# Emptying steps of a pipelined RWKV and FP4 layer: the x rounding moved in between the links of the gated values' rounding

## The chip, the cores and the metric

One NeuronCore of a Trainium2 chip runs the whole kernel. The metric is device time in microseconds of one launch. The engines are TensorE (PE), VectorE (DVE), ScalarE (ACT), GpSimd (POOL) and SyncE (SP), which issues the loads and stores. Each works off its own queue in program order, and semaphores tie them together.

## The reference

The input `x` is 4 sequences of 1024 tokens with 256 channels. Cut to what matters:

```
xx = shifted(x) - x
r, k, v = (x + xx * mix_r) @ W_r.T, (x + xx * mix_k) @ W_k.T, (x + xx * mix_v) @ W_v.T
g = sigmoid((x + xx * mix_g) @ W_g.T)
attn = linear recurrence over tokens of r, k, v with a decay per channel (16 heads of 16)
x1 = layernorm(x + layernorm(attn * g @ W_o.T) * gamma + beta)
xq = fp4(x1)                                  # blocks of 16 channels share max|x| / 6
h  = silu(xq @ fp4(w_gate).T) * (xq @ fp4(w_up).T)      # 704 wide
out = layernorm(x1 + fp4(h) @ fp4(w_down).T)
```

`fp4` divides by the block's scale, rounds to the eight magnitudes 0, 0.5, 1, 1.5, 2, 3, 4, 6 with the sign, and multiplies by the scale.

## The kernel before

The 4096 tokens are 32 tiles of 128 tokens (eight of a sequence). A software pipeline works on one stage of each of nine tiles per step: `run_tiles` calls each engine's `step` 40 times (g = 0 to 39), and in step g `tile(lag)` is tile g - lag, or None outside 0 to 31. The order inside a step is written out by hand for every engine, with the waits in front of each operation. There is no planner. The branch that runs here has `general` false, so `ffn` is 1.

The stages that matter here, by lag: 2 the scores (ACT copies them, POOL masks them in the next step, L410); 3 the attention output, gating by `gate_heads` (DVE L1355), the output projection (PE L919); 4 first norm (`norm1`), `centred`, `residual`, second norm (`norm2`), the roots on POOL (`rstd_of`, L392 and L404), and x1 on ACT (L597); 5 the rounding of x1 (`xgrid`) and its scaling on POOL (`scale_x`, L419); 6 the transposes of `xq` (PE L931), the split in a high and a low part (ACT L627, DVE L1324 `low_x`), gate and up matmuls (PE L855), SiLU (ACT L594) and the product (`gated`, DVE L1286); 7 the rounding of the product (`hgrid`), its scaling on POOL (`hq`, L462), its transposes (PE L956) and copies to SBUF (ACT L665, L667); 8 the down projection (PE L967), `add_x1` (DVE L1317), the last norm (`norm3`), its root, the output (ACT) and the store.

A rounding is a chain of seven links in `grid`, each waiting for the one before it: 0 block maximum (L1067), 1 scale (L1069), 2 reciprocal (L1071), 3 scaled values (L1073), 4 magnitude (L1076), 5 add (L1079), 6 subtract (L1081). For x1 the operands are 128x256 (scales 128x16), for the gated product 128x704 (scales 128x44). All the tiles that they use (`x_grid`, `x_mag`, `late`, which holds `hid`, `h_grid`, `h_mag` and `sig_h`) lie in SBUF.

Gate and up are done in halves of 352 columns, each in one bank: gate half 0, up half 0, gate half 1, up half 1 on PE. Up half 1 overwrites the bank that `gated(0)` reads, so PE waits for `hid_step` before it; `gated(1)` waits for up half 1. Link 0 of the next step's `hgrid` waits for `gated(1)`, and x link 0 waits for `x1_ready` of its tile, which ACT gives at the end of the step before.

A step is emptying (`draining`) when tiles 0 and 1 are None: steps 33 to 39. There `step` of DVE takes a list of its own, ACT does `gate(t, 1)` ahead of the `hq_t` copies and x1, and PE starts with the `xq` transposes and the down projection. x tiles 28 to 31 are rounded in steps 33 to 36. The last tile's product is rounded in two halves (`last_grid`, POOL L474). In an emptying step before the change, DVE does all x links behind `gated(0)`, and POOL's order is: masks, `xb` (L448), root 0, `hq`, root 2 (last norm), the last tile's halves, root 1 (x1), x scaling.

Of the kernel before, what the change touches and what calls it, by code (L numbers as in the profile page):

```python
# [35 lines left out]
TAB, LN, LN2, QN = 11, 8, 4, 7  # L36
# [20 lines left out]
def wait(eng, sem, value):  # L57

    if isinstance(value, int) and value <= 0:
        return  # L60
    eng.wait_ge(sem, value)
# [60 lines left out]
def build(nc, x, time_decay, mix_k, mix_v, mix_r, mix_g, w_r, w_k, w_v, w_g, w_o, gamma, beta,  # L122
          w_gate, w_up, w_down, out):
    with ExitStack() as ctx:
# [176 lines left out]
        def per_block(ap, n):  # L301
            return ap[:, 0:n].unsqueeze(2).broadcast_to([ap.shape[0], n, BLK])
# [63 lines left out]
        def _(pool):  # L366
# [20 lines left out]
            def rstd_of(t, i, general):  # L387
                wait(pool, ln_step if i < 2 else ln2_step, t.count(LN if i < 2 else LN2,
                                                                  (3, 8, 4)[i]))
                if i:  # L390
                    wait(pool, x1_ready if i == 1 else y_ready, t.count(1, 0))
                g.tensor_tensor(rstd[:, i:i + 1], veps[:, i:i + 1], neg_half, ALU.pow  # L392
                                ).then_inc((rstd_ready, x_rstd, y_rstd)[i], 1)
                if i:
                    ready = x_norm_ready if i == 1 else rstd2_ready
                    wait(pool, (rstd_ready, x_rstd, y_rstd)[i], t.count(1, 1))
                    if general:
                        g.tensor_tensor(nmr[:, i:i + 1], mv[:, i, 0:1], rstd[:, i:i + 1], ALU.mult
                                        ).then_inc((rstd_ready, x_mean, y_mean)[i], 1)
                        wait(pool, (rstd_ready, x_mean, y_mean)[i], t.count(1, 1))  # L400
                        g.tensor_tensor(nmr[:, i:i + 1], nmr[:, i:i + 1], minus, ALU.mult
                                        ).then_inc(ready, 1)
                    else:
                        g.tensor_scalar(nmr[:, i:i + 1], mv[:, i, 0:1], rstd[:, i:i + 1], -1.0,  # L404
                                        ALU.mult, ALU.mult).then_inc(ready, 1)
# [16 lines left out]
            def step(tile, general):  # L422
                ffn = 0 if general else FFN
                t = None if general else tile(3)
                if t is not None:
                    wait(pool, mixed, t.count(4, 12))
                    mask(t, 0)
                    mask(t, 1)
                    mask(t, 2)
                    mask(t, 3)  # L430
                t = tile(0)
                if t is not None:
                    wait(pool, x_t_ready, t.count(1, 1))
                    wait(pool, mixed, t.count(4, -4))
                    g.tensor_tensor(shift[:, t.c % 2], x_t[:, t.c % 2, :, 0:P],  # L435
                                    x_t[:, t.c % 2, :, 1:P + 1], ALU.subtract).then_inc(shifted, 1)
                    if not general and t.b == 0 and 1 <= t.c <= 4:
                        for n in range(2 * t.c - 2, min(2 * t.c, len(pieces))):
                            dequantize(n)
                        if t.c == 4:  # L440
                            pad_hidden()
                t = tile(4)
                if t is not None:
                    if t.first():
                        pool.wait_ge(norm_loaded, 16 * 2)
                    wait(pool, x_in[t.c], t.affine(16, 16))
                    wait(pool, ln_step, t.count(LN, 5 - 2 * LN))
                    g.tensor_tensor(xb[:, t.c % 2], x_tok[:, t.c], beta_b, ALU.add  # L448
                                    ).then_inc(xb_ready, 1)
                t = tile(4)  # L450
                if t is not None:
                    rstd_of(t, 0, general)
                drain = draining(tile, general)
                t = tile(7 + ffn)
                if t is not None and not drain:
                    rstd_of(t, 2, general)
                t = tile(6 + ffn)
                if t is not None and not (is_last(t) and drain):
                    wait(pool, hquant_step, t.count(QN, QN))
                    wait(pool, h_tr, t.count(1, -1))  # L460
                    nb = HID // BLK
                    g.tensor_tensor(blocks(hq[:, t.c % 2, 0:HID], nb), blocks(h_grid, nb),  # L462
                                    per_block(h_scale, nb), ALU.mult).then_inc(hq_ready, 1)
                t = tile(7 + ffn)
                if t is not None and drain:
                    rstd_of(t, 2, general)
                t = tile(5 + ffn)
                if is_last(t) and drain:
                    wait(pool, h_tr, t.count(1, -1))
                    nb = HH // BLK  # L470
                    for half in range(2):
                        pool.wait_ge(last_step[half], QN)
                        part = slice(half * HH, (half + 1) * HH)
                        g.tensor_tensor(blocks(hq[:, t.c % 2, part], nb), blocks(h_grid[:, part], nb),  # L474
                                        per_block(h_scale[:, half * nb:(half + 1) * nb], nb), ALU.mult
                                        ).then_inc(last_ready, 1)
                t = tile(4)
                if t is not None:
                    rstd_of(t, 1, general)
                if not general:  # L480
                    scale_x(tile(5), general)
                if general:
                    scale_x(tile(4), general)
# [562 lines left out]
        def _(dve):  # L1046
# [160 lines left out]
            def step(tile, general):  # L1207
# [28 lines left out]
                def hgrid(k):  # L1236
                    if t6 is None or is_last(t6) and not general:
                        return
                    if k == 0:
                        wait(dve, hid_step, t6.count(2, 2))  # L1240
                        wait(dve, hq_ready, t6.count(1, 0))
                    grid(k, hid, h_grid, HID // BLK, h_scale, h_inv, h_mag, hquant_step,
                         lambda i: t6.count(QN, i))
# [16 lines left out]
                def norm1(k):  # L1260
                    if t4 is not None:
                        if k == 0:
                            wait(dve, wo_done, t4.count(1, 1))
                        norm(k, B_S0[:, 0:C], 0, ln_step, t4, 1)
# [47 lines left out]
                def add_x1():  # L1312

                    if t7 is not None:
                        wait(dve, down_done, t7.count(1, 1))
                        wait(dve, y_ready, t7.count(1, 0))
                        v.tensor_tensor(u2, B_PA[:, 0:C], x1[:, t7.c], ALU.add).then_inc(ln2_step, 1)  # L1317
# [11 lines left out]
                def centred():  # L1329

                    if t4 is not None:
                        v.scalar_tensor_tensor(u1, B_S0[:, 0:C], mv[:, 0, 0:1], gamma_b,
                                               ALU.subtract, ALU.mult).then_inc(ln_step, 1)
# [60 lines left out]
                if draining(tile, general):  # L1394
                    if t2 is not None:
                        add_x1()
                    hgrid(0)
                    norm1(0)
                    hgrid(1)
                    norm1(1)  # L1400
                    hgrid(2)
                    norm1(2)
                    centred()
                    low_x()
                    hgrid(3)
                    residual()
                    gate_heads()
                    hgrid(4)
                    if t2 is None:
                        add_x1()  # L1410
                    norm2(0)
                    hgrid(5)
                    norm3(0)
                    norm2(1)
                    hgrid(6)
                    norm3(1)
                    norm2(2)
                    norm3(2)
                    next_state(0)
                    gated(0)  # L1420
                    last_grid(0)
                    xgrid(0)
                    next_state(1)
                    xgrid(1)
                    next_state(2)
                    for k in range(2, QN):
                        xgrid(k)
                    gated(1)
                    last_grid(1)
                    return  # L1430
# [144 lines left out]
```

## Time and profile before

| | us |
|---|---|
| three timed runs, median (lowest to highest) | 569.05 (568.41 to 571.27) |
| profiled execution | 567.12 |
| its span, first to last instruction | 565.3 |
| busy: TensorE matmuls | 515.4 (91%) |
| busy: VectorE | 507.7 (90%) |
| busy: GpSimd | 286.6 (51%) |
| busy: ScalarE | 260.1 (46%) |
| mean granted TensorE clock | 0.980 of full |

The shares are means over the whole span; a step in the full part takes about 15.4 us and is not touched by the edit. The emptying steps begin at about 495 us. A timeline row gives the start in us, the duration, the engine, the line, what is written and read, and in brackets how long the engine had been idle and who released it.

### The profile page before, as it was taken

How to read it: one execution, taken by the hardware profiler on the slowest of the kernel's cores; microseconds unless marked ns; L12 is line 12 of the kernel's file. 1: busy time of each engine (PE TensorE's matmuls, PEld its weight loads, DVE VectorE, ACT ScalarE, POOL GpSimd, SP SyncE). 2: the span in 40 equal slices, each digit the busy share in tenths (PEclk: the TensorE clock that was granted, in tenths of full speed). 3: DMA queues.
4: the chain of work that ended last, by engine and by line, in shares of the span. 5: the costliest groups of instructions: out<-in, count | busy, mean ns of one | idle time of the engine just before them, and what ended most of it. 6: DMA issues, size and time to landing. Idle time of an engine off the chain costs nothing.

```text
span 565.3 us, 14795 instructions
## 1 busy us (share of the span) xinstructions
PE 515.4 (91%) x5120; PEld 448.8 (79%) x5120; DVE 507.7 (90%) x1535; ACT 260.1 (46%) x614; POOL 286.6 (51%) x439
## 2 busy tenths in 40 slices
PE   2758789899999999999999999999999999988783
PEld 1647578788888888889888888888888988867672
DVE  7998578999999999999999999999999999799982
ACT  3426454445554444554554555444455454532221
POOL 3246453455566555555555555555565554554321
PEclk9969899999999999999999999999999999999997
DMA  7300000000000000000000000000000000000000
GB/s 211 129 1 2 11 11 10 1 22 20 20 21 21 20 20 20 5 18 20 20 20 21 20 20 20 20 21 20 11 12 20 10 11 12 12 10 11 10 20 23
DMA packets 14046, 13.14 MB, mean 23 GB/s; under 512 B 2576, under 2 KB 13712, under 8 KB 13968
## 3 DMA queue, kind: packets, MB, share of 16 engines
q1 hardware_dynamic: 13968, 12.13, 6.9%
q8 instruction: 45, 0.74, 0.5%
q14 instruction: 33, 0.27, 0.2%
HBM read 7.93 MB, written 4.19 MB: 21 GB/s over the span
## 4 chain that ended last, share of the span: by engine, by line
issue 45%; POOL 42%; DVE 8%; PE 3%; ACT 1%; POOLq 0%; DMA 0%; DVEq 0%; ACTq 0%
POOL scores L410 12%; POOL rstd L392 11%; POOL hq L462 8%; POOL nmr L404 4%; POOL shift L435 3%; POOL xb L448 2%; DVE mix L1222 2%; POOL xq L419 1%; PE bank L967 1%; PE bank L794 1%; DVE q_scale L1067 1%; ACT scores L589 1%; PE bank L919 1%; DVE hq L1079 0%; DVE hq L1073 0%
## 5 line engine op out<-in xcount | busy, mean ns | idle before, releaser
L589 ACT COPY scores<-bank 128x512 f32<-128x512 f32 x128 | 68.3, 593 | 72.0 <-PE bank L794 72.0
L462 POOL TENSOR_TENSOR hq<-late,h_scale 128x704 f32<-128x704 f32 x31 | 43.2, 1392 | 96.2 <-DVE late L1081 96.2
L967 PE MATMUL bank<-down_t,hq_t 128*128 128x256 f32 x384 | 89.9, 384 | 1.5 <-ACT hq_t L665 1.5
L410 POOL TENSOR_SCALAR_AFFINE_SELECT scores<-scores 128x512 f32<-128x512 f32 x128 | 80.8, 669 | 10.2 <-ACT scores L589 10.2
L967 PEld LDWEIGHTS bank<-down_t,hq_t 128*128 128x128 f32 x384 | 72.7, 193 | 10.8 <-issue 2.0
L1222 DVE SCALAR_TENSOR_TENSOR mix<-shift,mu,x_t 128x128 f32<-128x128 f32 x256 | 78.9, 355 | 1.3 <-POOL shift L435 1.3
L419 POOL TENSOR_TENSOR xq<-x_grid,x_scale 128x256 f32<-128x256 f32 x32 | 19.9, 622 | 113.0 <-DVE x_grid L1081 113.0
L392 POOL TENSOR_TENSOR rstd<-veps,neg_half 128x1 f32<-128x1 f32 x96 | 65.3, 690 | 19.0 <-DVE veps L1169 19.0
L855 PE MATMUL bank<-gu_hi,xq_hi 128*128 128x352 f32 x256 | 71.2, 359 | 2.6 <-DVE late L1286 2.6
L891 PE MATMUL bank<-mix,proj_t 128*128 128x128 f32 x512 | 66.1, 284 | 0.0
L891 PEld LDWEIGHTS bank<-mix,proj_t 128*128 128x128 f32 x512 | 61.1, 196 | 3.2 <-issue 1.1
L855 PE MATMUL bank<-gu_hi,xq_lo 128*128 128x352 f32 x256 | 61.7, 322 | 0.0
L855 PE MATMUL bank<-gu_lo,xq_hi 128*128 128x352 f32 x256 | 61.6, 322 | 0.0
L855 PEld LDWEIGHTS bank<-gu_hi,xq_hi 128*128 128x128 f32 x256 | 43.9, 188 | 14.8 <-issue 9.5
L1286 DVE TENSOR_TENSOR late<-late,bank 128x352 f32<-128x352 f32 x64 | 33.0, 516 | 19.6 <-PE bank L855 19.4
L532 ACT COPY x_t<-bank 128x256 f32<-128x256 f32 x32 | 12.0, 375 | 82.8 <-PE bank L704 82.8
L594 ACT ACTIVATE late<-bank 128x352 f32<-128x352 f32 x64 | 29.7, 465 | 37.6 <-PE bank L855 34.7
L794 PE MATMUL bank<-r_par,rv 32*128 32x256 f32 x512 | 37.6, 408 | 9.6 <-DVE kd L1389 7.3
L855 PEld LDWEIGHTS bank<-gu_lo,xq_hi 128*128 128x128 f32 x256 | 44.5, 188 | 0.0
L855 PEld LDWEIGHTS bank<-gu_hi,xq_lo 128*128 128x128 f32 x256 | 44.5, 188 | 0.0
L633 ACT COPY rv<-bank 128x512 f32<-128x512 f32 x32 | 18.8, 586 | 47.9 <-PE bank L891 47.9
L919 PE MATMUL bank<-proj_t,attn 128*128 128x256 f32 x128 | 34.2, 391 | 4.1 <-ACT scores L589 4.0
(128 smaller groups left out, 1131.4 us busy)
## 6 DMA issues: line engine op xcount, KB each, us to landing
x_tok<-in_L_attn_x_dram SPq DMA_DIRECT2D x32, 128.0 KB, 2.2
out_dram<-late_down SPq DMA_DIRECT2D x32, 128.0 KB, 1.7
late_down<-in_L_ffn_w_down_dram SPq DMA_DIRECT2D x1, 704.0 KB, 7.9
late<-in_L_ffn_w_gate_dram SPq DMA_DIRECT2D x1, 640.0 KB, 4.5
late<-in_L_ffn_w_up_dram SPq DMA_DIRECT2D x1, 640.0 KB, 6.6
scores<-in_L_attn_W_r_dram SPq DMA_DIRECT2D x1, 256.0 KB, 4.5
scores<-in_L_attn_W_v_dram SPq DMA_DIRECT2D x1, 256.0 KB, 4.6
scores<-in_L_attn_W_g_dram SPq DMA_DIRECT2D x1, 256.0 KB, 4.9
```

The costliest lines, as they stand in the source:

```text
L392: g.tensor_tensor(rstd[:, i:i + 1], veps[:, i:i + 1], neg_half, ALU.pow).then_inc((rstd_ready, x_rstd, y_rstd)[i], 1)
L410: g.affine_select(out=a, in_=a, compare_op=ALU.is_ge, fill=0.0, base=0, pattern=[[0, 4], [1, P]], channel_multiplier=-1).then_inc(s_masked, 1)
L462: g.tensor_tensor(blocks(hq[:, t.c % 2, 0:HID], nb), blocks(h_grid, nb), per_block(h_scale, nb), ALU.mult).then_inc(hq_ready, 1)
L589: s.copy(scores[:, t.c % 2, 4 * q:4 * q + 4, :], src).then_inc(s_moved, 1)
L594: s.activation(sig_h[:, i], B_GATE[:, 0:HH], ACT.Silu).then_inc(sig_ready, 1)
L794: mm = t_.matmul(s_bank[q][:, hf * 256:hf * 256 + 256], rv[rows, t.c % 4, 1, hf], r_par[rows, t.c % 2, hf].rearrange("p r n -> p (r n)"), ...
L855: mm = t_.matmul(b[:, 0:HH], x[:, t.c % 2, k], w[:, k, o + i * HH:o + (i + 1) * HH], start=(n == 0), stop=(n == len(parts) - 1))
L891: mm = t_.matmul(B_PA[:, o:o + P], proj_t[:, i, k, m * P:(m + 1) * P], mix[:, t.c % 2, i, k], start=(k == 0), stop=(k == KC - 1))
L919: mm = t_.matmul(B_S0[:, 0:C], attn[:, t.c % 2, k], proj_t[:, 4, k], start=(k == 0), stop=(k == KC - 1))
L967: mm = t_.matmul(B_PA[:, 0:C], hq_t[:, t.c % 2, j], down_t[:, j], start=(j == 0), stop=(j == NH - 1))
L1222: ins = v.scalar_tensor_tensor(mix[:, t0.c % 2, i, k], shift[:, t0.c % 2, k], mu[:, i, k:k + 1], x_t[:, t0.c % 2, k, 1:P + 1], ALU.mult, A ...
L1286: v.tensor_tensor(hid[:, i * HH:(i + 1) * HH], sig_h[:, i], B_UP[:, 0:HH], ALU.mult).then_inc(hid_step, 1)
```

## The change

Two edits, both only in emptying steps. On DVE the seven x links no longer follow `gated(0)` in a row; they stand one by one between the links of `hgrid`, and `gate_heads`, the norms and the state update shift a little against each other. On POOL the x scaling comes directly behind `hq`, then x1's root, then the last norm's root, then the last tile's halves. In full steps the order of both engines stays what it was.

```diff
@@ gpsimd step
                     g.tensor_tensor(blocks(hq[:, t.c % 2, 0:HID], nb), blocks(h_grid, nb),
                                     per_block(h_scale, nb), ALU.mult).then_inc(hq_ready, 1)
+                if drain:
+                    scale_x(tile(5), general)
+                t = tile(4)
+                if t is not None:
+                    rstd_of(t, 1, general)
                 t = tile(7 + ffn)
                 if t is not None and drain:
                     rstd_of(t, 2, general)
...
-                t = tile(4)
-                if t is not None:
-                    rstd_of(t, 1, general)
-                if not general:
+                if not general and not drain:
                     scale_x(tile(5), general)
@@ vector step, draining
                     hgrid(1)
                     norm1(1)
+                    xgrid(0)
                     hgrid(2)
                     norm1(2)
+                    xgrid(1)
                     centred()
+                    xgrid(2)
                     low_x()
                     hgrid(3)
                     residual()
+                    xgrid(3)
+                    hgrid(4)
+                    xgrid(4)
                     gate_heads()
-                    hgrid(4)
                     if t2 is None:
                         add_x1()
+                    hgrid(5)
+                    xgrid(5)
                     norm2(0)
-                    hgrid(5)
+                    hgrid(6)
+                    norm2(1)
                     norm3(0)
-                    norm2(1)
-                    hgrid(6)
+                    xgrid(6)
+                    norm2(2)
                     norm3(1)
-                    norm2(2)
+                    next_state(0)
                     norm3(2)
-                    next_state(0)
+                    next_state(1)
                     gated(0)
                     last_grid(0)
-                    xgrid(0)
-                    next_state(1)
-                    xgrid(1)
                     next_state(2)
-                    for k in range(2, QN):
-                        xgrid(k)
                     gated(1)
                     last_grid(1)
```

## Rows read from the trace of the kernel before

**Rows 1.** Windows, steps 33 to 36: length; PE, PEld, DVE, ACT, POOL busy; clock; DMA.
```profile
495.14:506.08 10.94, 8.68 (x111) 7.26 (x98) 10.77 (x36) 4.32 (x10) 4.41 (x7) 1.00 0.00 0
506.08:518.81 12.73, 10.69 (x112) 9.01 (x112) 11.78 (x34) 3.24 (x8) 8.14 (x13) 1.00 0.04 12
518.81:529.57 10.76, 7.80 (x44) 6.94 (x44) 10.52 (x33) 3.23 (x8) 5.16 (x9) 1.00 0.05 14
529.57:539.25 9.68, 7.80 (x44) 6.94 (x44) 9.13 (x23) 3.30 (x8) 2.83 (x5) 1.00 0.04 14
```

**Rows 2.** Timeline of PE: second up half, and the head of step 36.
```profile
526.44 0.59 PE L855 MATMUL bank<-gu_hi,xq_hi 128*128 128x352 f32 x2 [1.42 <-DVE late L1286]
...
529.87 0.44 PE L931 MATMUL bank<-ident,xq 128*128 128x128 f32 x2 [1.55 <-POOL xq L419]
```

**Rows 3.** Timeline, step 36: gate and up on PE, transposes, copies.
```profile
532.55 0.67 PE L855 MATMUL bank<-gu_hi,xq_hi 128*128 128x352 f32 x2
...
536.11 0.59 PE L855 MATMUL bank<-gu_hi,xq_hi 128*128 128x352 f32 x2 [0.33 <-DVE late L1286]
...
536.85 0.49 PE L855 MATMUL bank<-gu_hi,xq_lo 128*128 128x352 f32 x2
537.18 0.82 PE L956 MATMUL bank<-ident,hq 128*128 128x128 f32 x6
...
538.03 0.59 ACT L665 COPY hq_t<-bank 128x512 f32<-128x512 f32 x1 [1.75 <-PE bank L956]
```

**Rows 4.** Timeline of DVE (one row POOL), step 35 and two of step 36.
```profile
524.76 0.85 DVE L1081 SCALAR_TENSOR_TENSOR late<-late 128x704 f32<-128x704 f32 x1
...
525.70 1.39 POOL L462 TENSOR_TENSOR hq<-late,h_scale 128x704 f32<-128x704 f32 x1 [4.46 <-DVE late L1081]
...
525.86 0.52 DVE L1286 TENSOR_TENSOR late<-late,bank 128x352 f32<-128x352 f32 x1
526.30 0.41 DVE L1067 TENSOR_REDUCE x_scale<-x 128x16 f32<-128x256 f32 x1
...
528.68 0.42 DVE L1081 SCALAR_TENSOR_TENSOR x_grid<-x_mag,x_grid 128x256 f32<-128x256 f32 x1
529.02 0.51 DVE L1286 TENSOR_TENSOR late<-late,bank 128x352 f32<-128x352 f32 x1
...
535.54 0.52 DVE L1286 TENSOR_TENSOR late<-late,bank 128x352 f32<-128x352 f32 x1
```

**Rows 5.** Timeline, DVE and POOL: `s_half` free, then steps 33 and 34.
```profile
489.22 0.16 DVE L1374 TENSOR_TENSOR s_half<-s_part,half_decay 128x64 f32<-128x64 f32 x1
...
502.02 1.39 POOL L462 TENSOR_TENSOR hq<-late,h_scale 128x704 f32<-128x704 f32 x1 [4.47 <-DVE late L1081]
...
503.04 0.45 DVE L1374 TENSOR_TENSOR s_half<-s_part,half_decay 128x64 f32<-128x64 f32 x1
503.41 0.17 DVE L1069 TENSOR_SCALAR x_scale<-x_scale 128x16 f32<-128x16 f32 x1
...
508.66 0.73 POOL L448 TENSOR_TENSOR xb<-x_tok,beta_b 128x256 f32<-128x256 f32 x1
508.67 1.46 DVE L1073 SCALAR_TENSOR_TENSOR late<-late,h_inv 128x704 f32<-128x704 f32 x1
510.64 0.48 DVE L1342 SCALAR_TENSOR_TENSOR u<-u,rstd,xb 128x256 f32<-128x256 f32 x1 [0.51 <-POOL rstd L392]
```

**Rows 6.** Timeline of POOL, step 35: the x scaling.
```profile
529.20 0.62 POOL L419 TENSOR_TENSOR xq<-x_grid,x_scale 128x256 f32<-128x256 f32 x1
```

**Rows 7.** Windows at the end of the run, then PE's down projections.
```profile
551.50:554.10 2.60, 0.00 (x0) 0.00 (x0) 2.42 (x8) 0.00 (x0) 0.79 (x1) 1.00 0.00 0
...
556.00:559.50 3.50, 3.50 (x11) 2.73 (x10) 0.00 (x0) 0.20 (x1) 0.00 (x0) 0.52 0.13 42
...
530.14 2.76 PE L967 MATMUL bank<-down_t,hq_t 128*128 128x256 f32 x12
...
555.57 4.52 PE L967 MATMUL bank<-down_t,hq_t 128*128 128x256 f32 x12 [0.77 <-ACT hq_t L665]
```

## The prediction

> **What bounds the kernel now.** I first cut the seven emptying steps out of the page's long span, because only they run the edited code, and only four of them (I call them 33 to 36) hold an x rounding at all. In [rows 1] the reader sees one row per step, from the first link of the gated values' rounding to the next. VectorE (DVE) is busy 10.77 of 10.94 us, 11.78 of 12.73, 10.52 of 10.76 and 9.13 of 9.68, while TensorE (PE) has 1.9 to 3 us of slack in each step and GpSimd (POOL) more. So DVE's own queue sets the step; a wait of PE counts only if DVE later waits for PE. PE does wait 1.55 us for `xq` at the head of a step [rows 2], and that is the wait which the edit takes away. But step 36 runs on without it: what PE waits for next is DVE's first gated product (line 1286) [rows 3].
>
> The second thing to see is the order inside a DVE step [rows 4]: `gated(0)` at 525.86, then the seven x links (526.30 to 529.1), then `gated(1)` at 529.02, and 0.55 us later (529.57 by [rows 1]) the next step's first link. `gated(0)` to `gated(1)` is 3.16 us. Under those x links PE makes its return trip: `gated(0)` frees the bank of the up half, PE does six matmuls from 536.11 to 537.34 [rows 3] and only then may `gated(1)` read them. From 535.54, when `gated(0)` starts, to 537.38 that is 1.84 us, all of it hidden by the x rounding today.
>
> **The change, part by part.** Times are start to start on DVE. Two neighbours that don't depend on each other start about 0.08 us before the former's recorded end (0.41 long, 0.33 apart), a dependent one about 0.03 after it.
>
> 1. *x links go ahead of `gated(0)`.* Seven links of 0.41, 0.17, 0.25, 0.42, 0.29, 0.43 and 0.42 us [rows 4, 5] (0.17 is the second link's duration in the latter) less 7 x 0.08 are about 1.82 us a step, four steps: +7.3. In steps 33 to 35 the h chain is already filled with norms, so no gap absorbs them. In step 36 the h links stand almost alone; 0.27 us of gaps close there: -0.3.
>
> 2. *The x links leave the place behind `gated(0)`.* The interval falls from 3.16 to the return trip of 1.84: -1.32 in three steps, and -1.42 in step 33, which has 3.26. Sum -5.4. This is the cover that is gone: without the return trip the gain would have been up to 2.7 us a step. Parts 1 and 2 alone are +1.6.
>
> 3. *The last x link meets `hq` on GpSimd.* This is the largest term. POOL starts `hq` (L462, 1.39 us) 0.09 us after the last h link ends [rows 4]. In the new order the next DVE work is two small norm operations, of one input each, and then x link 6, which reads two SBUF tensors (`x_mag`, `x_grid`). The trace shows what such an operation does beside a POOL operation on data [rows 5]: `s_half`, 0.16 us when free, took 0.45 and ended 0.08 after `hq` did; h link 3, of two inputs, took 1.46 instead of 0.88 and ended 0.74 after `xb` did. Both look as if they had started about 0.1 before POOL's operation ended. So x link 6, wanted 0.35 us after the last h link (H), starts at H + 1.38: +1.03 in steps 33 to 35 and +1.10 in 36, where one norm operation less stands between: +4.2. Bounds: zero if the two rows have another cause, 1.2 a step (all of `hq`) above. I take 1.03, because two different pairs fit it within 0.1. In step 33 `s_half` now stands ahead of `gated(0)` and meets POOL's x scaling (0.62 [rows 6]): +0.35 by the same reading.
>
> The Trainium skill, "SBUF — State Buffer", section "Who interferes with whom", says that a DVE operation with two SBUF inputs contends with a GpSimd operation that reads SBUF, and that whichever starts first keeps the shared ports for its whole length while the other waits. By that rule term 3 stands as worked out, and the trace agrees with it (0.45 against 0.16).
>
> 4. *GpSimd's order.* The x scaling (0.62 [rows 6]) moves from behind two root pairs to ahead of them. `xq` is ready before PE wants it, which by [rows 1] buys nothing. x1's root comes later by the scaling but earlier by the swap with the last norm's; ScalarE reaches x1 only behind the `hq_t` copies anyway. Those follow PE's transposes. From `gated(0)` to the end of x1: 0.57 to PE's start, 1.07 to the transposes, 0.85 to the copy, 0.74 for the copies and 0.6 for x1 with its semaphore, 3.9 us [rows 3]. x link 0 is now wanted 1.84 + 0.55 + 1.36 = 3.75 us after `gated(0)` in step 35, and 1.84 + 0.55 + 1.05 = 3.44 in step 36, where it used to be far later: waits of 0.1 and 0.4, +0.5. What is queued behind this link are all later h links. Bounds 0 and 1.0.
>
> 5. *Step 34.* Today DVE stands idle in it for 0.95 us [rows 1], 0.51 of it for a root, and loses 0.58 in the blocked link [rows 5]. DVE now arrives later than today, but so do POOL's masks and `xb`; of the 1.5 I give back 1.0: -1.0 (bounds 0 and -1.5).
>
> 6. *Step 37* has no x rounding. Its `add_x1` waits 0.16 us for PE today; PE's down projection is tied to `gated(0)` of the step before by 3.3 us plus 2.7 of matmuls, and DVE is there 5.6 us after it: +0.3.
>
> 7. *PE's clock.* PE's down projection starts 3.3 us after `gated(0)` of the step before, gives way to the gate part 2.4 later, and three of its four quarters take 3.2 (from 532.55 to the idle time of 0.33 before 536.11 [rows 3]): 8.9 together. The next `gated(0)` comes 12.5 after the former and PE sees it 0.57 later. So in step 35 PE stands still for 4.2 us in one piece (3.2 without term 3), where today there are 1.42 and 1.55 [rows 2]. At the end of the run a pause of 2.6 us and a short burst were followed by the lower of the two levels (granted 0.52, 1.2 GHz), at which twelve down matmuls took 4.52 us in place of 2.76 [rows 7]. Six up matmuls and six transposes of 1.27 and 0.82 us at that ratio cost 0.75 + 0.5. One fall, in step 35, part of it beside other work: +0.9 (bounds 0 and, with falls in all four steps, 4).
>
> The sum is 7.3 - 0.3 - 5.4 + 4.2 + 0.35 + 0.5 - 1.0 + 0.3 = +6.0 and 0.9 for the clock: +6.9 us. The profiled execution took 567.12 us (span 565.3), so 574.0 by its own time. The three timed runs have their median at 569.05, 1.9 above it; on that scale the prediction is **576.0**, 1.2% slower. Everything outside steps 33 to 37 is untouched: the order of the full steps and the last tile's two halves stay.
>
> **The rivals.**
>
> *A: no blocking.* x link 6 runs at 0.42 us beside `hq`. Then term 3 goes, and the kernel is 1.5 us slower, 2.4 with the clock's fall, hence about **571.0**. For it: no x link stands beside `hq` today, and both blocked rows are of other shapes. Against it: [rows 5], twice.
>
> *B: faster.* PE's wait for `xq` (1.55 us in each of four steps, 6.1 in all) is on the path, and the return trip of the up half is short enough to be filled by `next_state` and by POOL's part. It decides from the point at which `gated(0)` is not later than today by more than 1.3 us. In that case dependency gaps of the x chain, 7 x 0.11 = 0.8 us a step, and a part of the wait go: about -4, **565.0**. Against it: seven links must pass DVE first, and DVE is full.
>
> *C: the clock falls often.* Pauses of 2.2 to 2.9 us stand in steps 33, 34 and 36 too, each as long as the one in [rows 7]. Three more falls at 0.9: **578.7**.
>
> **How the numbers follow.** Forecast 0.56, A 0.21, B 0.08, C 0.15. Less than 0.5% (2.8 us) is about what a measurement of this kernel can't tell from no change. A lies mostly inside it (569 to 572), B is faster, the rest slower. Faster 0.08, same 0.18, slower 0.74. The range runs from A's lower part, 570.5, to C's, 579.2; the likeliest case alone has 573.5 to 578.
>
> **What would show it.** In the trace after: x link 6 (line 1081, 128x256) longest of its kind, near 1.4 us against 0.42, and ending 0.3 us after `hq`; idle of DVE ahead of `gated(1)` of about 1.4 us ended by PE's line 855, four times; no wait of PE for `xq`; PE's wait ahead of the second up half up from 1.42 to some 4 us in step 35; steps 33 to 36 of 12.7, 13.0, 12.5 and 12 us. I am wrong if x link 6 keeps its 0.42 us, if `gated(1)` follows `gated(0)` without idle time, or if the steps get shorter than those of [rows 1].

## The result and the profile after

The changed kernel takes 577.68 us (573.1 to 579.2, 4 runs) against 569.02 (568.41 to 571.27) of the kernel before: ratio 1.0134, 95% interval 1.0105 to 1.0164. The forecast was 576.0 us, 1.2% slower. The changed kernel scatters over 6 us, the one before over 3.

First the windows of the profiled execution after, one line per emptying step, which answer to [rows 1] (step length, then busy us of PE, PEld, DVE, ACT, POOL, then granted clock and DMA):

```profile
498.11:510.73 12.62, 8.87 (x113) 7.38 (x100) 11.38 (x36) 3.23 (x7) 4.76 (x9) 1.00 0.00 0
510.73:523.77 13.04, 10.70 (x114) 9.06 (x113) 11.63 (x34) 3.04 (x7) 6.74 (x12) 1.00 0.04 11
523.77:536.82 13.05, 8.49 (x43) 7.61 (x42) 10.94 (x33) 3.04 (x7) 4.53 (x8) 0.92 0.04 12
536.82:548.71 11.89, 8.65 (x47) 7.66 (x46) 9.43 (x22) 3.04 (x7) 2.78 (x4) 0.93 0.03 12
```

The four steps take 50.60 us where they took 44.11, so 6.5 of the loss is here. I had written 12.7, 13.0, 12.5 and 12. Step 37 adds 1.4. The stretch behind it is 1.3 longer too (20.0 us against 18.8), but it takes 17.4 us in a second execution of the changed kernel and 19.7 in one with the kernel before's order, both further down, so nothing shows that this 1.3 belongs to the edit. The other 3.0 us of the two spans lie ahead of step 33, where both kernels issue the same instructions: step 33 begins at 498.11 here and at 495.14 there, and at 498.41 in the execution with the kernel before's order. Most of it is there early: one and the same block maximum of VectorE starts at 103.90 us in the kernel before and at 106.65 here. That is scatter of the start-up part and no effect of the edit. Steps 33 to 37 alone are 7.9 us longer.

Step 35 on DVE and POOL answers to [rows 4] (the links' lines are two higher after the edit). The reader should look at x link 6 (line 1083, `x_grid`), at what POOL does beside it, and at the idle time ahead of the second product:

```profile
531.78 1.38 POOL L462 TENSOR_TENSOR hq<-late,h_scale 128x704 f32<-128x704 f32 x1 [5.11 <-DVE late L1083]
...
532.02 1.42 DVE L1083 SCALAR_TENSOR_TENSOR x_grid<-x_mag,x_grid 128x256 f32<-128x256 f32 x1
...
533.52 0.62 POOL L419 TENSOR_TENSOR xq<-x_grid,x_scale 128x256 f32<-128x256 f32 x1 [0.36 <-DVE x_grid L1083]
...
533.75 0.52 DVE L1288 TENSOR_TENSOR late<-late,bank 128x352 f32<-128x352 f32 x1
536.26 0.52 DVE L1288 TENSOR_TENSOR late<-late,bank 128x352 f32<-128x352 f32 x1 [1.99 <-PE bank L857]
```

The link takes 1.42 us where it took 0.42, and ends 0.28 after `hq`. It is 1.42, 1.43, 1.42 and 1.50 in the four steps. After `gated(0)` DVE has nothing left to do and stands for 1.20, 1.31, 1.99 and 1.32 us.

PE around the same place, and the granted clock of two stretches of it (the columns of the windows as above):

```profile
534.33 0.73 PE L857 MATMUL bank<-gu_hi,xq_hi 128*128 128x352 f32 x2 [4.02 <-DVE late L1288]
534.85 0.79 PE L857 MATMUL bank<-gu_lo,xq_hi 128*128 128x352 f32 x2
...
536.03 1.48 PE L958 MATMUL bank<-ident,hq 128*128 128x128 f32 x6
```
```profile
531.00:534.30 3.30, 0.00 (x0) 0.00 (x0) 3.24 (x10) 0.00 (x0) 2.16 (x3) 1.00 0.00 0
534.50:538.00 3.50, 3.43 (x14) 2.96 (x14) 1.59 (x3) 0.46 (x1) 1.18 (x4) 0.52 0.00 0
```

PE's pause grew from 1.42 [rows 2] to 4.02 us, its clock fell to 1.2 GHz behind it, and six transposes took 1.48 us in place of 0.82 [rows 3]. The next step's head shows where that lands (first row), and the head of step 37, behind a second fall, the same once more:

```profile
538.93 0.42 DVE L1069 TENSOR_REDUCE x_scale<-x 128x16 f32<-128x256 f32 x1 [1.01 <-ACT x L599]
...
550.82 0.42 DVE L1326 TENSOR_TENSOR xq_lo<-bank,xq_hi 128x256 fp32r<-128x256 f32 x1 [0.54 <-ACT xq_hi L629]
...
553.64 0.42 DVE L1319 TENSOR_TENSOR late_down<-bank,x 128x256 f32<-128x256 f32 x1 [1.03 <-PE bank L969]
```

Only a part of these waits is the clock's: in a kernel whose clock stays up (fitted fillers, below) the first is 0.38, the second 0.18 and the third 0.16 us. PE no longer waits for `xq`: its transposes at 537.30 follow those of h without a gap. The wait that the edit removes is gone, and it was not the one that counted.

### The profile page after: what moved, and what is told of

It reads as the page before. It is cut to its first block, busy times and chain, and to the rows that moved or that the text cites. A ratio compares the mean times of both kernels' runs of the same rounds, so it can differ in the third digit from the quotient of the medians.

```text
span 577.4 us, 14795 instructions
## 1 busy us (share of the span) xinstructions
PE 522.7 (91%) x5120; PEld 454.3 (79%) x5120; DVE 510.3 (88%) x1535; ACT 259.6 (45%) x614; POOL 284.3 (49%) x439
## 4 chain that ended last, share of the span: by engine, by line
issue 45%; POOL 40%; PE 6%; DVE 3%; ACT 2%; SPq 1%; DMA 1%; POOLq 0%; DVEq 0%; ACTq 0%
POOL scores L410 11%; POOL rstd L392 11%; POOL hq L462 7%; POOL nmr L404 4%; POOL shift L435 3%; POOL xb L448 2%; POOL xq L419 1%; PE bank L893 1%; DMA scores<-in_L_attn_W_o_dram 1%; PE bank L969 1%; PE bank L796 1%; PE bank L733 1%; DVE mix L1224 1%; ACT scores L591 1%; PE bank L864 1%
## 5 line engine op out<-in xcount | busy, mean ns | idle before, releaser
L969 PE MATMUL bank<-down_t,hq_t 128*128 128x256 f32 x384 | 92.0, 391 | 3.3 <-ACT hq_t L667 3.3
L969 PEld LDWEIGHTS bank<-down_t,hq_t 128*128 128x128 f32 x384 | 73.9, 196 | 14.2 <-issue 5.0
L1224 DVE SCALAR_TENSOR_TENSOR mix<-shift,mu,x_t 128x128 f32<-128x128 f32 x256 | 80.9, 364 | 1.6 <-POOL shift L435 1.6
L635 ACT COPY rv<-bank 128x512 f32<-128x512 f32 x32 | 18.8, 586 | 48.3 <-PE bank L893 48.3
L796 PEld LDWEIGHTS bank<-r_par,rv 32*128 32x128 f32 x512 | 24.5, 192 | 18.8 <-issue 18.1
```

The source lines that it names most:

```text
L796: mm = t_.matmul(s_bank[q][:, hf * 256:hf * 256 + 256], rv[rows, t.c % 4, 1, hf], r_par[rows, t.c % 2, hf].rearrange("p r n -> p (r n)"), ...
L969: mm = t_.matmul(B_PA[:, 0:C], hq_t[:, t.c % 2, j], down_t[:, j], start=(j == 0), stop=(j == NH - 1))
L1224: ins = v.scalar_tensor_tensor(mix[:, t0.c % 2, i, k], shift[:, t0.c % 2, k], mu[:, i, k:k + 1], x_t[:, t0.c % 2, k, 1:P + 1], ALU.mult, A ...
```

## The experiments

My theory has three parts: x link 6 is blocked by `hq` (lock); the return trip of the second up half lies open behind `gated(0)` (return trip); and the pauses that both make lower PE's clock (clock). The rivals: the number of links on DVE, GpSimd's order, or chance.

The table holds the step lengths of all profiled executions, from the start of the gated values' first link to the next (step 37: to the last tile's first one), and the ratios to the kernel before. Each row of steps is one execution, each ratio comes from all of them, and the two don't always agree: the execution of "scaling ahead of `hq`" is the fastest of its six (570.81 us), that of "x link 6 behind" one of the two slowest of its twelve (573.39).

| kernel | 33 | 34 | 35 | 36 | 37 | sum | ratio (95%) |
|---|---|---|---|---|---|---|---|
| before | 10.94 | 12.73 | 10.76 | 9.68 | 7.29 | 51.4 | 1 |
| changed | 12.62 | 13.04 | 13.05 | 11.89 | 8.66 | 59.3 | 1.0134 (1.0105 to 1.0164) |
| changed, again | 12.59 | 14.67 | 13.24 | 11.88 | 7.42 | 59.8 | 1.0098 (1.0070 to 1.0127) |
| scaling ahead of `hq` | 11.59 | 12.83 | 11.67 | 10.84 | 7.69 | 54.6 | 1.0072 (1.0048 to 1.0097) |
| x link 6 behind `gated(0)` | 11.63 | 12.76 | 11.75 | 10.59 | 7.42 | 54.2 | 1.0019 (1.0002 to 1.0036) |
| own bank | 12.62 | 11.63 | 11.33 | 10.02 | 6.85 | 52.5 | 1.0018 (0.9997 to 1.0038) |
| fillers, too long | 12.59 | 14.69 | 14.03 | 11.54 | 7.42 | 60.3 | 1.0144 (1.0117 to 1.0171) |
| fillers, fitted | 12.59 | 13.04 | 12.37 | 11.27 | 7.42 | 56.7 | 1.0070 (1.0051 to 1.0089) |
| GpSimd's order only | 10.94 | 14.18 | 11.59 | 10.91 | 7.65 | 55.3 | 1.0080 (1.0057 to 1.0104) |
| VectorE's order only | 12.34 | 14.32 | 13.90 | 12.19 | 8.28 | 61.0 | 1.0127 (1.0106 to 1.0148) |
| split links | 10.39 | 12.88 | 11.06 | 10.45 | 7.44 | 52.2 | 1.0001 (0.9982 to 1.0020) |
| own bank, links 5 and 6 last | 11.29 | 12.63 | 10.10 | 9.38 | 8.01 | 51.4 | 1.0003 (0.9984 to 1.0022) |
| before, own bank | 10.94 | 12.73 | 10.77 | 9.68 | 7.29 | 51.4 | 1.0011 (0.9989 to 1.0032) |
| link 6 behind, own bank | 11.62 | 11.80 | 10.49 | 9.75 | 7.55 | 51.2 | 1.0002 (0.9983 to 1.0021) |

**The lock, by GpSimd alone.**

```diff
+                if drain:
+                    scale_x(tile(5), general)
                 t = tile(6 + ffn)
                 if t is not None and not (is_last(t) and drain):
                     wait(pool, hquant_step, t.count(QN, QN))
...
-                if drain:
-                    scale_x(tile(5), general)
```

> The changed kernel with one edit on GpSimd: in an emptying step the x scaling stands ahead of hq, not behind it. So no GpSimd operation reads SBUF while x link 6 runs, and nothing on VectorE is moved. Theory (x link 6 is blocked by hq): the link is back at 0.42 us from 1.42, gated(0) comes about 1.0 us earlier in each of four steps, hq ends later by the scaling and the link (about 1.4 us after the last h link, but only 0.3 after the second up half), so 3 to 4 us less than the changed kernel: about 574, ratio to the kernel before 1.006 to 1.009. Rival (the link is long for another cause, or VectorE's length doesn't set the step): the link stays near 1.4 us and the time is the changed kernel's or up to 1 us above it, 577 to 579.

573.55 us (570.81 to 575.66), ratio 1.0072. VectorE's code is untouched, and its link is short again (step 35):

```profile
529.00 0.40 DVE L1083 SCALAR_TENSOR_TENSOR x_grid<-x_mag,x_grid 128x256 f32<-128x256 f32 x1
529.47 0.62 POOL L419 TENSOR_TENSOR xq<-x_grid,x_scale 128x256 f32<-128x256 f32 x1 [5.84 <-DVE x_grid L1083]
...
530.05 1.39 POOL L464 TENSOR_TENSOR hq<-late,h_scale 128x704 f32<-128x704 f32 x1
```

So the lock is shown: 1.0 us a link, steps 33 and 36 each 1.03 to 1.05 shorter. Step 34 is only 0.21 shorter, where a wait of 0.51 us for a root comes back, as in the kernel before. The whole gain is 3 to 4 us (against 576.62 and 577.68). The rival (the link is long for another cause) falls.

**The lock and the return trip, by one link.**

```diff
-                    xgrid(6)
                     norm2(2)
...
                     gated(0)
                     last_grid(0)
+                    xgrid(6)
                     next_state(2)
```

> The changed kernel with only the last x link moved: from ahead of gated(0) to directly behind it. Theory: it misses hq or meets only its end, and it lies in the return trip, so gated(0) comes 1.3 us earlier in each of four steps while gated(1) still follows 1.8 us after it: 5 us less, TensorE's pauses shorter too, 571 to 573, ratio 1.004 to 1.007. Rival (link number on VectorE is what counts, wherever it stands): at most 1 us less. If both the lock and the return trip count, this is more than the other kernel that moves only GpSimd's scaling gives.

570.45 us (569.82 to 573.46), ratio 1.0019: 6 to 7 us less than the changed kernel, for one link in another place, and more than the 5 that I expected. The link reads 0.41, 0.53, 0.53 and 0.61 us, so it meets only `hq`'s end (in step 33 `s_half` meets it instead, 0.77 us), and `gated(1)` still comes 1.84 after `gated(0)` in step 34. That the count of links is what costs is refuted.

**The return trip.** Second up half of tiles 28 to 31 (steps 34 to 37) in a bank that is free in these steps; VectorE's product reads it there:

```diff
-                for b, o in ((B_GATE, 0), (B_UP, HID)):
+                own = i == 1 and own_bank(t)
+                for b, o in ((B_GATE, 0), (B_S1 if own else B_UP, HID)):
...
-                        wait(pe, hid_step, t.count(2, i))
+                        wait(pe, hid_step, t.count(2, 0 if own else i))
```

> The changed kernel, but the second up half of tiles 28 to 31 (steps 34 to 37) goes into a PSUM bank that is free by then, so TensorE doesn't wait for gated(0) and gated(1) doesn't wait for the return trip. Theory (the return trip that nothing fills any more is on the path): gated(0) to gated(1) falls from 1.83 to 0.44 us in steps 34 to 36, TensorE's long pause ahead of the second up half is split up, so 4 us less and perhaps 1 to 2 more where the clock stays up: 572 to 574, ratio 1.005 to 1.009. Step 33 keeps its return trip. Rival (the return trip is covered by something else, such as hq, which the next step's first link waits for): less than 1 us.

570.4 us (568.78 to 574.25), ratio 1.0018. The link is still blocked, but both products now follow each other:

```profile
530.44 1.41 DVE L1089 SCALAR_TENSOR_TENSOR x_grid<-x_mag,x_grid 128x256 f32<-128x256 f32 x1
...
532.15 0.95 DVE L1294 TENSOR_TENSOR late<-late,bank 128x352 f32<-128x352 f32 x2
```

I expected 572 to 574. It gave more, and in the trace the transposes of h don't wait behind the second up half either: step 36 begins its x link without a wait for x1. The control is the same bank in the kernel before:

> The kernel before, unchanged in its order, with the bank of its own for the second up half. Theory: there the return trip is hidden by the x links (3.16 us against 1.84), so the bank gains nothing: within 0.5 us of the kernel before, ratio 0.999 to 1.001. Rival (the bank helps by itself, through an earlier transpose of h and an earlier x1, and not by closing the gap that the change opened): 1.5 us or more faster.

569.96 us (567.96 to 574.3), ratio 1.0011 (0.9989 to 1.0032), and step for step the lengths of before. Where the x links cover the trip, the bank is worth nothing.

**The clock.** The first attempt put 12 and 8 matmuls of 128x256 into PE's pause of steps 35 and 36:

> The changed kernel with matmuls of no use on TensorE in its long pause ahead of the second up half: 12 of 256 columns in step 35, 8 in step 36, into a free bank. Nothing else waits for them. Theory (the lower clock level after that pause costs a part): the granted clock stays at its upper level in steps 35 to 37, gated(0) to gated(1) of step 35 goes from 2.51 to 1.83 us, the waits for x1 and the down projection at the head of steps 36 and 37 shrink by 1 to 1.5 together, so 1.5 to 3 us less than the changed kernel, 575 to 576, and less scatter between executions. Rival (the clock's share is noise of the one profile): the same time as the changed kernel, 577 to 578, or more, since the fillers delay the second up half.

577.65 us (576.0 to 579.61), ratio 1.0144. This run decides nothing: its first group was too long.

```profile
530.68 5.34 PE L857 MATMUL bank<-proj_t,ident 128*128 128x256 f32 x24
535.67 0.67 PE L867 MATMUL bank<-gu_hi,xq_hi 128*128 128x352 f32 x2
```

The profile counts 24, two instructions for each of the twelve fp32 matmuls. The up half came 1 us late, and the clock fell in steps 33 and 34, where no filler stood. Fitted, with `fillers` giving 4, 3, 8 and 6 for tiles 27 to 30:

```diff
+                    if b is B_UP and i == 1:
+                        for _ in range(fillers(t)):
+                            t_.matmul(B_T[:, 0:C], ident, proj_t[:, 0, 0], start=True, stop=True)
```

> The first filler run missed its aim: an fp32 matmul is two passes, so 12 of them took 5.3 us in a pause of 4.0 and delayed the second up half, and the clock fell in steps 33 and 34, which had none. Now 4, 3, 8 and 6 fillers in steps 33 to 36, at 0.44 us each, 1.8 in a pause of 2.2, 1.3 in 1.8, 3.5 in 4.0 and 2.6 in 2.9, into the bank of the x transposes, which is free there. Theory (the lower clock costs a part of the loss): full clock from 498 to about 560 us, gated(0) to gated(1) 1.83 us in all four steps, no wait over 0.5 at the heads of steps 36 and 37, 1.5 to 3 us less than the changed kernel. Rival (the clock's falls lie where nothing waits): the same time within 0.5 us.

573.88 us (573.19 to 574.87), ratio 1.0070. It does more work and is 2.7 us faster than the changed kernel beside it (576.62), and its six runs lie within 1.7 us where that one's lie within 4.9. The size is not sharp: between the means it is 2.0 us, and the intervals of the two ratios overlap. The steps agree with it: 56.7 us against 59.3 and 59.8. So do the executions of the changed kernel among themselves: in both sets the one with the highest mean clock (0.979 and 0.982) is the fastest, 573.1 and 572.94 us, and both are about as fast as the fillers. The granted clock is 1.00 over steps 33 to 36 against 0.94 after the change:

```profile
498.00:553.00 55.00, 48.81 (x329) 42.29 (x326) 48.32 (x131) 14.61 (x33) 20.18 (x33) 1.00 0.03 11
```
```profile
498.00:553.00 55.00, 40.77 (x326) 34.91 (x325) 46.74 (x129) 14.07 (x32) 18.81 (x31) 0.94 0.03 10
```

**The changed kernel again.**

> The changed kernel once more, unaltered, beside the three others on the same chip. It gives the scatter of its executions. Theory: 1.0 to 1.5% above the kernel before. If TensorE's clock falls in other steps in this execution than in the first (there: 35, 36, the end), the waits of those steps grow by 0.7 and that of the next head by up to 1.

576.62 us (572.94 to 577.79), ratio 1.0098. The clock fell in steps 33, 34 and 35 in this execution, not in 35 and 36; step 34 is 14.67 instead of 13.04, step 37 is 7.42 instead of 8.66. Which step pays differs, the sum hardly. The first of these falls, in the columns of the windows, stands behind a pause of PE of 2.23 us, which is as long as the one of step 33 in the first execution, where the clock stayed up:

```profile
510.40:513.90 3.50, 3.16 (x13) 2.52 (x11) 3.28 (x11) 2.11 (x5) 3.08 (x6) 0.51 0.00 0
```

**The two edits apart.**

> Only the VectorE edit: GpSimd's order is that of the kernel before (roots, then x scaling). Theory: the cost is all on VectorE, in x link 6 beside hq and in the open return trip. The roots take GpSimd to about 1.7 us after gated(0), the x scaling to 2.4, when TensorE has just done the transposes, so this equals the changed kernel within 0.7 us, 577 to 578, 1.2 to 1.5% slower than before. Rival (GpSimd's order carries a part of the loss): over 1.5 us less than the changed kernel.

577.69 us (576.49 to 578.76), ratio 1.0127, within 1.1 us of the whole change on the same chip (I had written 0.7). The loss comes with VectorE's order.

> Only the GpSimd edit: VectorE's order of the kernel before, GpSimd's order of the changed one (x scaling directly behind hq, then x1's root, then the last norm's). Theory: with the x links still behind gated(0), the x scaling waits for them, 3.2 us after gated(0), and both roots queue behind it. ScalarE's x1 and output then come 2 to 3 us later, and behind them in its queue the copy of xq's high part, for which low_x and TensorE's next gate part wait. So 1 us a step in three steps: 2 to 4 us slower than before, 571 to 573. Rival (the GpSimd order is the useful or harmless part): within 1 us of the kernel before.

574.88 us (572.42 to 576.05), ratio 1.0080: as the theory says in kind, and more than its 2 to 4 us. In VectorE's old order the scaling waits for the x links with both roots behind it, and the chain goes over ScalarE's queue, as these rows of step 34 show:

```profile
511.48 0.43 DVE L1326 TENSOR_TENSOR xq_lo<-bank,xq_hi 128x256 fp32r<-128x256 f32 x1 [0.73 <-ACT xq_hi L629]
514.87 0.49 DVE L1344 SCALAR_TENSOR_TENSOR u<-u,rstd,xb 128x256 f32<-128x256 f32 x1 [1.80 <-POOL rstd L392]
```

The second row I had missed: POOL's masks and `xb` of step 34 queue behind the roots too. So the two edits don't add up. GpSimd's order costs 0.8% with the old list of VectorE and nothing measurable with the new one.

**Looking for something better.** Links 0 to 2 late among the h links, 3 to 6 behind `gated(0)`, GpSimd doing `hq`, x1's root, scaling, last root:

> The x links are shared out: links 0, 1 and 2 stand late among the h links, links 3 to 6 with next_state behind gated(0), where they fill the return trip; GpSimd does hq, x1's root, the x scaling, the last norm's root. Theory: 0.6 us of links ahead of gated(0), and 2.0 to 2.2 us behind it in place of 3.16, so 0.4 to 0.6 us a step less than the kernel before in four steps, and no pause of TensorE long enough to lower its clock: 1.5 to 2.5 us faster than before, ratio 0.9955 to 0.998. Rival (interleaving costs in itself, as link 0 waits for x1 and the order on GpSimd matters): no faster than before, 1.000 to 1.005.

570.0 us (567.05 to 572.74), ratio 1.0001 (0.9982 to 1.0020). Step 33 gains 0.55 as worked out. Step 34 loses 0.15 (a wait of 1.20 for the first root), steps 35 and 36 lose 0.3 and 0.8 (PE pauses 2.52 us, its clock falls, and `low_x` waits 1.29 for ScalarE's copy).

> As the kernel with a bank of its own for the second up half (steps 34 to 37), with gated(1) straight behind gated(0) and x links 5 and 6 behind gated(1), where hq has ended, links 0 to 4 among the h links; GpSimd's order hq, x1's root, x scaling, last norm's root. Theory: neither the lock nor the return trip is left in steps 34 to 36, only VectorE's own length: 1 us a step less than before, 2.5 to 4 us faster than before, ratio 0.993 to 0.996. Step 33 keeps an open return trip and may lose 0.5. Rival (x1's way over TensorE, ScalarE is the next bound): waits for x1 at link 0 of 0.5 to 1 us a step, and no gain, 0.998 to 1.002.

570.26 us (567.68 to 572.81), ratio 1.0003 (0.9984 to 1.0022). Steps 35 and 36 gain 0.7 and 0.3 us; step 33 loses 0.35 and step 37 0.7, where `low_x` waits 1.02 for the copy that stands behind ScalarE's output.

> Both remedies at once on the changed kernel: x link 6 behind gated(0), as in the kernel that moves it alone (ratio 1.0019), and the second up half of tiles 28 to 31 in a bank of its own, as in the other (1.0018). Theory: the two causes are separate but share one place. With link 6 behind it, gated(0) to gated(1) is 0.9 us in steps 34 to 36, the link ends about where hq does, and TensorE has no pause that lowers its clock. From the step lengths of the two kernels I expect 11.6, 11.5, 10.5, 9.6 and 6.9 us in steps 33 to 37, 50 in all against 51.4 of the kernel before: 1 to 2 us faster than before, ratio 0.996 to 0.999. Rival (each remedy alone has already moved the bound to hq, the copies and x1, so that the second finds nothing): equal to the kernel before or to the one-remedy kernels, 1.000 to 1.002.

569.33 us (567.17 to 572.91), ratio 1.0002 (0.9983 to 1.0021). The rival holds. Each remedy alone takes away 6 to 7 us, both together at most 1 more than one of them, which the intervals can't tell from nothing. Against what I expected, PE's clock still fell once, at the turn from step 35 to 36 (granted 0.51 from 530.1 to 533.6 us), behind a pause of 2.12 us. What is left in its trace is a wait for x1, of 0.33 us in step 35 and, behind that fall, of 1.00 in step 36:

```profile
532.80 0.42 DVE L1075 TENSOR_REDUCE x_scale<-x 128x16 f32<-128x256 f32 x1 [1.00 <-ACT x L604]
```

No version beats the kernel before by a measurable amount.

## Why the prediction was right, step by step

- *What bounds the kernel* (VectorE's queue sets the step, PE's wait for `xq` doesn't): shown. The wait is gone and the steps are longer.
- *Parts 1 and 2* (+1.6: seven links ahead of `gated(0)`, return trip of 1.84 behind it): `gated(0)` to `gated(1)` is 1.85, 1.83, 2.51 and 1.83 us after. Step 36 of the kernel with the scaling ahead of `hq`, which has only these two parts and its head's wait, is 1.16 longer than before: 0.2 for the two parts and 1.00 for the wait, which here also holds a fall of the clock. The bank gives the trip back.
- *Part 3* (+4.2 and 0.35: the lock): 1.42, 1.43, 1.42 and 1.50 us against 0.42, so 1.0 to 1.1 each; `s_half` 0.47 against 0.22 with VectorE's order only, where no x scaling runs beside it. The two rows of [rows 5] carried this estimate to within 0.1. The rule of the Trainium skill ("SBUF — State Buffer", section "Who interferes with whom") holds for the pair of x link 6 and `hq`, which the kernel before didn't have: removing the GpSimd operation, not touching the link, makes it short. The prediction's remark under rival A that no x link stood beside `hq` was not so: in step 35 of the kernel before, `hq` ends at 527.09, and x link 1, at 526.75, takes 0.37 us in place of 0.17 and ends 0.03 after it; in steps 34 and 36 it takes 0.37 too. That row spoke against A as well.
- *Part 4* (x1 late at the head of 35 and 36 by 0.1 and 0.4): with the clock kept up, 0 and 0.38. (Its five durations add up to 3.83 us, not 3.9, which changes neither wait by a tenth.)
- *Part 5* (step 34 gives back 1.0): step 34 is 13.04; I wrote 13.0.
- *Part 6* (+0.3 in step 37): with the clock kept up 7.42 against 7.29, +0.13, and not where I put it: `add_x1` waits 0.16 us as before, and `low_x` 0.18 for ScalarE's copy.
- *Part 7* is the mis-sized term. I put 0.9 us on one fall of the clock in step 35. The fitted fillers show 2.7 between the medians, and 2.6 and 3.1 in step lengths against the two executions of the changed kernel. Falls come in two or three of the four steps, and one in step 36 runs on into step 37, where `add_x1` waits 1.03 for a down projection of 3.71 us instead of 2.76. Rival C (several falls, 578.7) had the right mechanism; the measured 577.68 lies between it and the forecast. The execution shown of the kernel before also started step 33 1 to 3 us earlier than the others do, which the median took care of.
- *The sum*: parts 1 to 6 were put at +6.0 us, and with the clock kept up steps 33 to 37 are 5.3 longer (the medians differ by 3.8). The clock was put too low by about 2 us. The two errors lean against each other, so a part of how near 576.0 comes to the two medians of the changed kernel (577.68 and 576.62) is luck.
- *Rival A* (no blocking, 571.0) fell with the trace; *rival B* (faster) had the right idea, that closed gaps and a filled trip can pay, but the best of the orders only equals the kernel before.

The share of each cause can't be added up: one moved link or one bank removes 6 to 7 us, more than the lock alone (3 to 4). A part of that is the clock, which falls less often but not never: in the executions shown it falls two and three times in steps 33 to 37 of the changed kernel and once in each of these two (0.51 from 531.9 us with x link 6 behind, 0.50 from 533.8 with the own bank). The five executions of the own bank with a mean clock of 0.979 take 568.8 to 570.5 us, the six at 0.971 or less 570.3 to 574.3. How the 6 to 7 us divide is not shown.

## What to carry to other kernels

An order that looks slack, such as a chain of dependent links in a row, may be what hides another engine's answer: before moving it away, measure the time from the operation that releases the other engine to the one that needs its answer (here 1.84 us). Before an operation with two SBUF inputs is moved beside a GpSimd operation, add GpSimd's whole remaining duration to it. And where a change opens pauses on TensorE, price the clock as its own term, in every step that gets a pause.

## What I had not expected of the hardware

PE's pauses ahead of the second up half are 2.23, 1.79, 4.02 and 2.90 us in steps 33 to 36 of one execution of the changed kernel, and the granted clock fell behind the last two; in another they are 2.23, 1.78, 3.86 and 2.53, and it fell behind the first three. So in these two the length of a pause alone does not say whether the clock falls. The changed kernel's times spread over 5 to 6 us, the fillers' over 1.7; matmuls of no use took 2.7 us off the median. An fp32 matmul of 128x256 counts as two instructions of 0.22 us in the profile (24 for 12, 5.34 us), which spoilt one experiment.
